# A mixture-of-experts transformer layer: plain writes for the last expert, an early exponential table, one tensor for PSUM, row maxima at even distances

## What is computed

```python
x = x + tanh(g_xattn[0]) * xattn(_layernorm(x), ctx, ctx, W_q, b_q, W_k, b_k, W_v, b_v, W_o, b_o)
h = _layernorm(x) ; h = _layernorm(h, ln_g, ln_b).reshape(Tn, D)
top_vals, top_idx = top_k(h @ Wr, 2) ; gates = softmax(top_vals)
xe = zeros((7, 732, D)).at[idx, pos_c].set(h[tok], mode='drop')
a, b = einsum('ecd,edf->ecf', xe, W1), einsum('ecd,edf->ecf', xe, W3)
ye = einsum('ecf,efd->ecd', silu(a) * b, W2)
routed = zeros((Tn, D)).at[tok].add(ye[idx, pos] * gate)
shared = silu(h @ W1s) * (h @ W3s) @ W2s
x = x + tanh(g_ffn[0]) * (routed + shared)
```

## Time and profile before

| | us |
|---|---|
| median of three runs | 865.51 |
| lowest and highest | 865.47, 865.97 |
| profiled execution | 866.94 |
| its span | 865.1 |
| PE busy | 824.0 (95%) |
| DVE busy | 588.9 (68%) |
| ACT busy | 387.8 (45%) |
| POOL busy | 322.2 (37%) |

### The profile page before, as it was taken

One profiled execution on the slowest core, in us unless ns is written; L12 is line 12 of the kernel. 1 busy time (PEld: TensorE's weight loads), 2 busy tenths in 40 slices (PEclk: granted clock), 3 DMA queues, 4 the chain that ended last, 5 costly groups with the idle time before them and its releaser, 6 DMA issues.

```text
span 865.1 us, 14600 instructions
## 1 busy us (share of the span) xinstructions
PE 824.0 (95%) x5228; PEld 719.4 (83%) x5228; DVE 588.9 (68%) x1292; ACT 387.8 (45%) x717; POOL 322.2 (37%) x247
## 2 busy tenths in 40 slices
PE   8888999999999999999999999999999999999990
PEld 7474858868778688686788899999999999999990
DVE  7587788787788776888877666575656657574340
ACT  3647363373452632635344454454535445453330
POOL 7454103150031320302326306638183663814244
PEclk9999999999999999999999999999999999999996
DMA  8441411324004222031033523333444333321111
GB/s 266 128 122 28 123 37 42 84 50 121 14 25 121 51 65 69 25 99 37 1 122 97 170 71 98 85 99 61 110 98 101 83 87 101 60 62 20 19 19 19
DMA packets 93601, 66.86 MB, mean 77 GB/s; under 512 B 54726, under 2 KB 80508, under 8 KB 93544
## 3 DMA queue, kind: packets, MB, share of 16 engines
q1 hardware_dynamic: 39288, 54.27, 22.0%
q0 software_dynamic: 53088, 10.30, 8.7%
q10 hardware_dynamic: 1168, 1.57, 0.7%
HBM read 37.38 MB, written 14.27 MB: 60 GB/s over the span
## 4 chain that ended last, share of the span: by engine, by line
PE 80%; issue 4%; DVE 3%; ACT 2%; POOL 1%; DVEq 0%; ACTq 0%; POOLq 0%
PE bank L1633 20%; PE bank L1635 20%; PE bank L1634 20%; PE bank L1919 3%; PE bank L1920 2%; PE bank L1921 2%; PE bank L1773 2%; PE bank L1767 2%; DVE row_max L1303 2%; PE bank L1734 2%; ACT float_data L1123 1%; PE bank L1961 1%; PE bank L1866 1%; PE bank L1945 1%; PE bank L1640 1%
## 5 line engine op out<-in xcount | busy, mean ns | idle before, releaser
L1633 PE MATMUL bank<-split_operands 128*128 128x366 f32 (+4 forms) x1104 | 364.0, 330 | 1.6 <-POOL split_operands L940 0.9
L1635 PE MATMUL bank<-split_operands 128*128 128x366 f32 (+4 forms) x1104 | 359.5, 326 | 0.0
L1634 PE MATMUL bank<-split_operands 128*128 128x366 f32 (+4 forms) x1104 | 359.4, 326 | 0.0
L1633 PEld LDWEIGHTS bank<-split_operands 128*128 128x128 f32 (+1 forms) x1104 | 205.8, 186 | 17.2 <-issue 5.9
L1635 PEld LDWEIGHTS bank<-split_operands 128*128 128x128 f32 (+1 forms) x1104 | 205.5, 186 | 10.4
L1634 PEld LDWEIGHTS bank<-split_operands 128*128 128x128 f32 (+1 forms) x1104 | 205.9, 187 | 8.3
L1039 POOL DMA_INDIRECT out<-float_data,scatter_now x42 | 125.7, 2992 | 185.8 <-DVE float_data L1596 97.6
L1616 DVE TENSOR_TENSOR hidden<-bank,float_data 128x366 f32<-128x366 f32 x112 | 60.5, 540 | 114.0 <-PE bank L1635 114.0
L1222 ACT ACTIVATE float_data<-bank 128x366 f32<-128x366 f32 x112 | 53.5, 478 | 113.6 <-PE bank L1635 110.5
L1219 ACT CAST split_operands<-hidden 128x366 fp32r<-128x366 f32 x112 | 55.7, 497 | 68.3 <-DVE hidden L1616 68.3
L1014 POOL DMA_INDIRECT float_data<-z_scratch,gather_now x42 | 72.9, 1736 | 17.4 <-issue 16.2
(11 more groups left out here) (173 smaller groups left out, 1109.2 us busy)
## 6 DMA issues: line engine op xcount, KB each, us to landing
float_data<-in_L_ffn_W SPq DMA_DIRECT2D x21, 1024.0 KB, 8.7
split_operands<-split_operands SPq DMA_DIRECT2D x88, 128.0 KB, 2.3
float_data<-in_x SPq DMA_DIRECT2D x8, 512.0 KB, 4.4
z_scratch<-float_data SPq DMA_DIRECT2D x8, 512.0 KB, 3.1
out<-float_data SPq DMA_DIRECT2D x7, 512.0 KB, 2.8
split_operands<-split_operands SPq DMA_DIRECT2D x8, 192.0 KB, 3.8
float_data<-in_L_ffn_W1s SPq DMA_DIRECT2D x2, 512.0 KB, 8.8
float_data<-in_L_ffn_W3s SPq DMA_DIRECT2D x2, 512.0 KB, 7.4
```

The costliest lines, as they stand in the source:

```text
L1633: pe.matmul(o, lhs[0], rhs[0], start=first, stop=False)
L1634: pe.matmul(o, lhs[0], rhs[1], start=False, stop=False)
L1635: return pe.matmul(o, lhs[1], rhs[0], start=False, stop=last)
```

## The change

1. The last expert's second half. From its third hidden tile on, PE takes only output tile 0 between the ups. After the last up come tile 0's rest, tile 1 and tile 2, one after the other. The hidden tiles 4 to 7 go to a buffer of their own (`late`), since all must stay. POOL gathers the half's rows of `out` (three indirect gathers, new step `rows_of_last`) behind its wait for the expert before and ahead of this expert's scatters. DVE multiplies by the gate and adds the gathered row in one instruction. POOL's last three indirect transfers write without adding. In all experts POOL waits for each output tile by itself.
2. In the first period the queries' stacks of heads for the first pairs (ranks 0 and 1, four high transfers on ACT's queue, two low on SP's) have a semaphore of their own with the maxima of pairs 0 and 1. The four high transfers of ranks 2 and 3 move to SP, behind the keys, and the low ones of ranks 2 and 3 between the two transfers of the maxima.
3. `exp_table`: an exponential of 128 × 1 into an unused column right after up(7), and in the second period after up(2) too. It stands ahead of the cast of hidden tile 7.
4. PSUM is one tensor of eight banks. The two exponentials of a pair become one of 77 × 1024, and the three reductions of a set become two, of 924 and 308 columns.
5. In a period the logits' transposes move between the two halves of up(5), with `pick` in odd ones; down(3) and down(4) are cut so that parts of them stand between the sets of maxima. In the second period down(3) is cut around the transposes.

```diff
@@ first period: @@
     do("stack", b)
     do("keys", b)
+    do("stack_rest", b)
@@ second_period @@
     up(2)
+    do("exp_table", b)
     do("logits", f)
     do("first_scores", b)
...
-    down(3)
+    down(3, 0, 2)
     do("logits_T", b)
+    down(3, 2, TT)
...
     up(7)
+    nxt("exp_table")
@@ period @@
     do("logits", b)
-    up(5)
+    do("up_a", f, 5)
     do("logits_T", b)
     if odd:
         do("pick", b, 0)
-    else:
+    do("up_b", f, 5)
+    if not odd:
         do("one_hots", f, 0)
         do("one_hot_values", f, 0)
-    down(3)
+    down(3, 0, 2)
     nxt("maxima", 1)
     up(6)
     nxt("maxima", 2)
-    down(4)
+    down(3, 2, TT)
+    down(4, 0, 3)
     nxt("maxima", 3)
+    down(4, 3, TT)
...
     up(7)
+    nxt("exp_table")
@@ buffers @@
+    late = ar(96, 2, NF - RING, HALF)
...
-    bank = [ctx.enter_context(nc.psum_tensor(f"bank{j}", [P, 512], F32)) for j in range(8)]
+    banks = ctx.enter_context(nc.psum_tensor("bank", [P, 8, 512], F32))
+    bank = [banks[:, j] for j in range(8)]
...
+    def hidden_at(e, n):
+        if e.at(E - 1) and n % NF >= RING and n >= NF:
+            return late[:, :, n % NF - RING]
+        return gT[:, :, n % RING, 0:HALF]
@@ SP, stack_maxima @@
-            for r0, r1, loaded in ((0, 2, sig["qst_loaded"]), (2, NPAIR, sig["qst_rest_loaded"])):
+            first, rest = ("qst0_loaded", "qst0_rest_loaded") if b.at(0) else ("qst_loaded", "qst_rest_loaded")
+            for r0, r1, loaded in ((0, 2, sig[first]), (2, NPAIR, sig[rest])):
                 sp.dma_start(qst[96:112, r0:r1, :].bitcast(F32),
                              mtr[:, :].bitcast(F32).unsqueeze(1).broadcast_to([H, r1 - r0, N])).then_inc(loaded, 16)
+                if b.at(0) and r0 == 0:
+                    stack_first_lo((2, 3), sig[rest])
@@ POOL @@
+        def rows_of_last(e):
+            pool.wait_ge(sig["xeT_ready"], E * 2 * KD)
+            apart(pool)
+            for t in range(NR // 2, NR):
+                pool.indirect_dma_start(xg[1][0:RT, t, :], None, out2,
+                                        bass.IndirectOffsetOnAxis(ap=gidx[e.c][0:RT, t:t + 1].bitcast(U32), axis=0))\
+                    .then_inc(sig["rows_gathered"], 16)
+            pool.wait_ge(sig["rows_gathered"], 16 * (NR // 2))
...
-                pool.wait_ge(sig["acc_done"], T // P + (e.n * 2 + half + 1) * (NR // 2))
-                apart(pool)
                 for t in range(half * NR // 2, (half + 1) * NR // 2):
+                    pool.wait_ge(sig["acc_done"], T // P + e.n * NR + t + 1)
+                    apart(pool)
+                    added = half == 1 and e.at(E - 1)
...
-                                            compute_op=ALU.add).then_inc(sig["scattered"], 16)
+                                            **({} if added else {"compute_op": ALU.add})).then_inc(sig["scattered"], 16)
@@ ACT @@
-            for w in range(2):
-                last = act.activation(prob[p % 4][0:SK, w], bank[2 * (p % 2) + w][0:SK, :], ACT.Exp, scale=DH ** -0.5)
-            last.then_inc(sig["exp_done"], 1)
+            act.activation(prob[p % 4][0:SK], banks[0:SK, 2 * (p % 2):2 * (p % 2) + 2], ACT.Exp, scale=DH ** -0.5)\
+               .then_inc(sig["exp_done"], 1)
...
+        def exp_table(b):
+            act.activation(warm[:, :], tgx[:, :], ACT.Exp)
@@ DVE @@
-            for j, (h0, h1) in enumerate(MAX_HEADS):
-                last = dve.tensor_reduce(mx[:, t, h0:h1],
-                                         bank[max_banks(b, t)[j]][:, 0:(h1 - h0) * SK].rearrange("p (h t) -> p h t", t=SK), AX.X, ALU.max)
+            first, _, third = max_banks(b, t)
...
+            dve.tensor_reduce(mx[:, t, 0:h0].rearrange("p (j h) -> p j h", j=2),
+                              banks[:, first:first + 2, 0:n].rearrange("p j (h t) -> p j h t", t=SK), AX.X, ALU.max)
+            last = dve.tensor_reduce(mx[:, t, h0:h1], bank[third][:, 0:(h1 - h0) * SK].rearrange("p (h t) -> p h t", t=SK),
+                                     AX.X, ALU.max)
...
+                if added:
+                    y = dve.scalar_tensor_tensor(out=ye[0:RT, r, :], in0=bank[4 + t][0:RT, 0:D], scalar=gw[e.c][0:RT, r:r + 1],
+                                                 in1=xg[1][0:RT, r, :], op0=ALU.mult, op1=ALU.add)
@@ PE, the last expert @@
+            def down_tiles_in_turn():
+                down(2 * NF - 2, (0,))
+                for n in range(NF, 2 * NF - 3):
+                    down(n, (1,))
+                down(2 * NF - 1, (0,))
+                for n in range(2 * NF - 3, 2 * NF):
+                    down(n, (1,))
+                for n in range(NF, 2 * NF):
+                    down(n, (2,))
...
-                if n >= 2:
+                if n >= 2 + NF and e.at(E - 1):
+                    down(n - 2, (0,))
+                elif n >= 2:
                     down(n - 2)
```

136 lines of the change are left out of this document (85 added, 51 removed).

## The result

The changed kernel takes 852.56 us (median of four runs, 850.94 to 852.70), the kernel before 865.74 beside it. The ratio is 0.9843 (0.9826 to 0.986). The forecast was 845.6 with a range of 841 to 852: the direction was right, the gain of 13.2 us was two thirds of the 19.9 that were forecast, and the time lies 0.6 us outside the range.

What follows compares the result with a forecast made beforehand. TensorE, fully busy once the experts run, was taken as the bound; gains lay in its earlier waits and the tail. First period 0.7, scoring 3.25, maxima 4.3, tail 11.6: 19.9 us off, median 845.6, range 841 to 852.

Steps and rivals of the forecast that it cites:

- Tail: Behind TensorE's last matmul: new tile order and plain writes move the span's end from 865.1 to 853.5, 11.6 us gained.
- the step that put the end on the adds' data: Tail: adds' data end at 849.3, then three plain writes of 0.9 us each and 1.6 give 853.5.
- Scoring: Attention turns 1 to 7: merged exponentials and early table gain 3.25 us of 4.1 listed, from 0 to 4.5.
- the table: Scoring: the early load fits ScalarE's idle gap ahead of the last cast, gaining 0.9 us in turns 2 and 6.
- The merged exponential: Scoring: 1024 columns take 1.03 us, 0.92 apart against 0.97; eight pairs gain 0.43, of which 0.35 is left.
- Maxima: Row maxima and logits' transposes in the periods: TensorE's waits removed, 4.3 us gained, from 2 to 5.
- First period: Fewer transfers on ScalarE's queue let first scores start about 27; with merged reductions 0.7 us gained, from −1 to 2.
- The median: Whole kernel: the sum is made on the profiled span, 865.1, and the difference taken off the median, 865.51.
- upstream absorbed: Rival, ahead of the experts: VectorE stands next in every chain, upstream gains 3 instead of 8.3: 851; chance 0.2 with late gathers.
- Plain writes that drain like adds: Rival, tail: a plain write's row takes an add's time, so the tail gains nothing: 857; chance 0.1.
- Late gathers: Rival, tail: previous expert's scatters land at 828, not 822.6; tail gains 6, not 11.6: 851; chance 0.2 with upstream absorbed.
- A slower exponential across two banks: Rival, scoring: one exponential across two banks costs ScalarE more than two single ones; at 1.35 us a pair 873; chance 0.04.

Runs made afterwards that it cites:

- nowait: The changed kernel without GpSimd's wait for the gathered rows ahead of the last expert's scatter-adds: 853.25 us.
- best: The changed kernel with matmuls of no use filling TensorE's waits in the first two periods, and no GpSimd wait for gathered rows before the last scatter-adds: 850.80 us.
- unroll: best_stack with the token stage's loop of two over two periods written out as four periods: 850.05 us, against 850.52 for best_again beside it.
- best_stack: best with the first period's stacks of queries issued as before the change: 850.21 us.
- best_again: best_stack once more, as the base of unroll on the same chip: 850.52 us.

## Why the prediction was wrong

Of the 6.7 us missed, 1.65 are in the scoring, 1.25 in the maxima, 0.8 in the tail, 0.3 were given back behind 433 us, where I didn't look further, and some 2.8 lie in the step from the profiles to the medians.

**Tail: near in size, wrong in one step of its chain.** 11.6 forecast, 10.8 in the two profiles, and 9.8 against the mean of the eight tails. GpSimd's times were right: 1.7 us a plain write, its end 3.7 us behind TensorE's, where at most 5 was said. Wrong was the step that put the end on the adds' data, with 0.9 us for each plain write behind them. Without any adds in the way (nowait, best) the data still run for about 5 us after GpSimd's end, as they do in the changed kernel. What the adds ahead do cost is 1.2 us on the mean, half of it through GpSimd's start. That the forecast end of the tail lay within 0.8 of the profile's, by another chain, was in part luck. The packets were judged nearly right: in best all that moved behind 838 us came to 843 packets, so at most 281 for a plain write against 992 for an add.

**Scoring: the mechanism right, both sizes too large.** 3.25 forecast, 1.6 measured. For the table, 0.9 us in each of turns 2 and 6 became 0.4. The step that failed took the time that ScalarE wins for time that TensorE wins: the third pair's scores stand behind down(7), and ScalarE waits for them. The merged exponential measured 1.017 us long and 0.92 apart, as worked out, but of 0.43 a turn 0.14 on the mean came through and not 0.35. Turns 1 and 4 gained nothing, as forecast. For turn 4 I named VectorE's chain; unroll shows that in the changed kernel the loop's jump stands in it with 1.59 us, of which 0.6 to 0.9 reached TensorE.

**Maxima: 3.05 for 4.3.** The odd periods were nearly right (0.73 and 0.70 against 0.86); the even ones gave 0.32 against 0.56, and the second 0.65 against 0.9. I had taken each listed loss as removed, though the margin that I had worked out was 0.03 us; waits of 2.0 and 0.7 us are left.

**First period: right number, wrong content.** 0.65 against 0.7. But the profile before had the clock's fall at 30 to 34 us and the one after had none; the second set of scores began later (31.81 against 31.16), and best, best_stack and best_again do not tell the edit's own worth from nothing. The agreement of 0.65 with 0.7 is luck.

**The median.** I took one profiled execution of before for the sum and moved the result by a constant. Some 2.8 of the 6.7 us missed lie there: by 1.2 the profile before was longer than its median, by 1.6 the profile after shorter than its own. The second is mostly the tail: 9.9 us in this profile, 10.9 on the mean of eight. What I did not foresee is this spread, nor that a turn whose gain I counted as nothing could turn into a loss in some runs, by an idle lump and the clock. Among the rivals, upstream absorbed (851) came nearest by its number, but not by its reason: upstream brought 5.0 and not 3, and VectorE's list took the gain in turns 1 and 4 alone, the turns that the forecast had named.

**The rivals that fell.** Plain writes that drain like adds: from GpSimd's end 6 to 8 us and not 9.4. Late gathers: the adds start 12.0 us ahead of TensorE's end, where 12.9 were forecast, less than 1 us late. A slower exponential across two banks: 0.92 a pair against 0.97. The Trainium skill's 2.66 us for a table switch (ScalarE: Activation LUTs, What ACT_TABLE_LOAD costs): here the load takes 1.28, and the next activation follows at 340.30, 0.01 after its end; the measurement decides.
